# A GRU behind a long convolution on one core: one of four channel chunks of the convolution goes from VectorE to ScalarE and GpSimd

## What is computed

```python
def reference(x, cond_2048, L1_cond_W_ih, L1_cond_W_hh, L1_cond_b_ih, L1_cond_b_hh):
    ...
    def cell(h, x):
        gi = x @ W_ih + b_ih
        gh = h @ W_hh + b_hh
        i_r, i_z, i_n = jnp.split(gi, 3, axis=-1)
        h_r, h_z, h_n = jnp.split(gh, 3, axis=-1)
        r = jax.nn.sigmoid(i_r + h_r)
        z = jax.nn.sigmoid(i_z + h_z)
        n = jnp.tanh(i_n + r * h_n)
        h_new = (1.0 - z) * n + z * h
        return (h_new, h_new)
    ...
    x = x + _L0_cond_ref(x, cond_2048[:, None, :])
    x = x + _L1_cond_ref(cond_2048, x, L1_cond_W_ih, L1_cond_W_hh, L1_cond_b_ih, L1_cond_b_hh)
    return x
```

## Time and profile before

| | |
|---|---|
| median of 3 runs | 1025.09 us (1024.73 to 1025.14) |
| profiled execution, span | 1023.1 us |
| TensorE busy | 1015.2 us, 99% |
| VectorE busy | 865.7 us, 85% |
| ScalarE busy | 398.5 us, 39% |
| GpSimd busy | 237.9 us, 23% |
| granted TensorE clock, mean | 1.000 |

### The profile page before, as it was taken

One profiled execution on the slowest core, in us unless ns is written; L12 is line 12 of the kernel. 1 busy time (PEld: TensorE's weight loads), 2 busy tenths in 40 slices (PEclk: granted clock), 3 DMA queues, 4 the chain that ended last, 5 costly groups with the idle time before them and its releaser, 6 DMA issues.

```text
span 1023.1 us, 58102 instructions
## 1 busy us (share of the span) xinstructions
PE 1015.2 (99%) x24838; PEld 808.1 (79%) x24838; DVE 865.7 (85%) x2851; ACT 398.5 (39%) x1816; POOL 237.9 (23%) x784
## 2 busy tenths in 40 slices
PE   8999999999999999999999999999999999999997
PEld 5878888888787888888888888888888888888875
DVE  7788888888898888888888898888888887777555
ACT  5334333433433343333434333333433343333433
POOL 3222222222222222222222222222222222222222
PEclk9999999999999999999999999999999999999999
DMA  8721001010100101001010010101001000000000
GB/s 297 72 35 39 19 21 31 15 36 19 29 25 12 35 19 34 24 11 36 15 39 19 15 36 11 39 19 28 22 15 35 14 29 16 11 29 4 20 19 13
DMA packets 66994, 32.07 MB, mean 31 GB/s; under 512 B 44464, under 2 KB 65584, under 8 KB 66736
## 3 DMA queue, kind: packets, MB, share of 16 engines
q1 hardware_dynamic: 66304, 28.25, 10.8%
q10 hardware_dynamic: 432, 0.11, 0.0%
HBM read 19.86 MB, written 8.49 MB: 28 GB/s over the span
## 4 chain that ended last, share of the span: by engine, by line
PE 97%; issue 1%; POOL 1%; DVE 0%; DMA 0%; ACT 0%; DVEq 0%; POOLq 0%
PE pg L334 65%; PE pg L324 32%; POOL tz L283 1%; PE pcv L362 0%; DMA cnd<-cond 0%; DVE hp L570 0%; DVE gn L549 0%; POOL nzh L296 0%; DVE an L557 0%; POOL cpad L273 0%; POOL nzh L280 0%; POOL cpad L275 0%; POOL rz L278 0%; POOL zcp L279 0%; ACT nzh L472 0%
## 5 line engine op out<-in xcount | busy, mean ns | idle before, releaser
L334 PE MATMUL pg<-whh,hp 128*32 128x192 f32 x16368 | 713.0, 326 | 2.2 <-ACT whh L461 1.1
L334 PEld LDWEIGHTS pg<-whh,hp 128*32 128x32 f32 x16368 | 531.2, 110 | 137.7 <-DVE hp L570 4.2
L324 PE MATMUL pg<-wih,x 128*32 128x192 f32 x8192 | 381.3, 326 | 0.0
L296 POOL TENSOR_TENSOR nzh<-rz,hp 128x32 f32<-128x32 f32 x512 | 158.2, 309 | 780.1 <-ACT rz L467 780.1
L467 ACT ACTIVATE rz<-gt 128x64 f32<-128x64 f32 x512 | 136.3, 266 | 483.7 <-DVE gt L545 458.9
L324 PEld LDWEIGHTS pg<-wih,x 128*32 128x32 f32 x8192 | 265.5, 110 | 65.8
L512 DVE SCALAR_TENSOR_TENSOR x<-xb,cnd,x 128x512 f32<-128x512 f32 (+1 forms) x420 | 294.8, 702 | 7.9
L570 DVE TENSOR_TENSOR_SCAN hp<-zcp,nzh 128x96 f32<-128x96 f32 x512 | 173.6, 339 | 41.6 <-ACT nzh L472 41.3
L545 DVE STREAM_TRANSPOSE gt<-pg 128x128 f32<-128x128 f32 x512 | 160.2, 313 | 49.4 <-PE pg L334 42.0
L557 DVE TENSOR_TENSOR_SCAN an<-rz,gn 128x64 f32<-128x64 f32 x512 | 149.2, 291 | 51.9 <-ACT rz L467 51.7
L472 ACT ACTIVATE nzh<-an 128x32 f32<-128x32 f32 x512 | 120.6, 236 | 126.9 <-DVE an L557 126.9
(11 more groups left out here) (47 smaller groups left out, 47.4 us busy)
## 6 DMA issues: line engine op xcount, KB each, us to landing
xb<-x SPq DMA_DIRECT2D x96, 94.0 KB, 2.0
out<-x SPq DMA_DIRECT2D x60, 128.0 KB, 1.9
wih<-w_ih SPq DMA_DIRECT2D x4, 768.0 KB, 8.0
whh<-w_hh SPq DMA_DIRECT2D x4, 768.0 KB, 14.6
xw<-x SPq DMA_DIRECT2D x24, 64.0 KB, 3.5
xb<-x SPq DMA_DIRECT2D x16, 62.0 KB, 1.9
tz<-taps SPq DMA_DIRECT2D x12, 64.0 KB, 3.5
xs<-x SPq DMA_DIRECT2D x1, 512.0 KB, 4.7
```

What stands on the lines that cost most here:

```text
L296: pool.tensor_tensor(nzh[:, f, ::2, :, 1], chunks(rz[:, f, 1, :, 1]), h_of(t - 1, slice(f * CH, (f + 1) * CH)), ALU.mult).then_inc(s_zh[f], 1)
L324: i = pe.matmul(pg[m % Q][f][D * j:D * (j + 1), RZ:END], x1_of(c, 2 * m, 2 * m + 2), wih[:, c, :, :].rearrange("p (g k) (j d) -> p j g k d ...
L334: i = pe.matmul(pg[t // 2 % Q][f][D * j:D * (j + 1), 0:IN], hp[:, t % 2, 2 * c + 1 - t % 2:2 * c + 3 - t % 2, :, 1].rearrange("p u b -> p ...
```

## The change

Chunk 3 (`SHARED = C - 1`) of the seven windows leaves VectorE. ScalarE makes the product of the shifted x by the tap's column into one of two new buffers `prod` (`weigh`, line 480 of the changed kernel), and GpSimd adds it into x1 (`gather`, line 313). There are 16 of each per window, so 112 of each in all, and VectorE keeps 48 per window. `weigh` stands at the end of a step on ScalarE, behind the seeds; `gather` at the end of a step on GpSimd, one step later (`t - 1`). TensorE's products wait for the sums as well. The fourth chunk's input is loaded at the window's start, the other three a little more spread out. In the changed kernel `recur` is line 361, `product` 351, `scan_h` 611, z·h 319, `add_out` 298, `long` 553.

```diff
+        prod = [sb(f"prod{i}", [P, W2 * B]) for i in range(2)]
...
-        EVERY = [(lag, c) for c in range(C) for lag in range(K)]
+        EVERY = [(lag, c) for c in range(C - 1) for lag in range(K)]
+        SHARED = C - 1
...
-            at = SPANS[k][0] + W2 // C * c
+            at = SPANS[k][0] + (0 if c == SHARED else W2 // SHARED * c)
...
                 if i == 0 and k >= 2:
-                    sp.wait_ge(s_long, len(EVERY) * (k - 2) + K * (c + 1))
+                    if c == SHARED:
+                        sp.wait_ge(s_prod, K * (k - 1))
+                        sp.wait_ge(s_sum, K * (k - 2) + 1)
+                    else:
+                        sp.wait_ge(s_long, len(EVERY) * (k - 2) + K * (c + 1))
...
+            def gather(k, lag):
+
+                q = K * k + lag
+                a, b = LONG[k]
+                n = (b - a) * B
+                pool.wait_ge(s_prod, q + 1)
+                if lag == 0 and b > KEEP:
+                    for s in range(max(a - KEEP, 0) // TB, (b - 1 - KEEP) // TB + 1):
+                        pool.wait_ge(s_out[s], 16 * C)
+                if lag:
+                    pool.wait_ge(s_sum, q)
+                o = x1_of(SHARED, a, b)
+                now = window(k)[:, SHARED, (K - 1) * B:(K - 1) * B + n]
+                pool.tensor_tensor(o, prod[lag % 2][:, 0:n], o if lag else now, ALU.add).then_inc(s_sum, 1)
...
                     if f == 0 and t:
                         add_out(t - 1)
+                for k, steps in enumerate(SPANS):
+                    for lag in share(K, steps, t - 1):
+                        gather(k, lag)
...
                         pe.wait_ge(s_long, len(EVERY) * sum(a <= 2 * m for a, _ in LONG))
+                    pe.wait_ge(s_sum, K * sum(a <= 2 * m for a, _ in LONG))
...
+            def weigh(k, lag):
+
+                q = K * k + lag
+                n = (LONG[k][1] - LONG[k][0]) * B
+                if lag == 0:
+                    act.wait_ge(s_xb[k][SHARED], 16 * PIECES)
+                if q >= 2:
+                    act.wait_ge(s_sum, q - 1)
+                act.activation(prod[lag % 2][:, 0:n], window(k)[:, SHARED, (K - 1 - lag) * B:(K - 1 - lag) * B + n],
+                               ACT.Copy, scale=cnd[:, SHARED, K - 1 - lag:K - lag]).then_inc(s_prod, 1)
...
                         seed(t // 2 + Q, f)
+                for k, steps in enumerate(SPANS):
+                    for lag in share(K, steps, t):
+                        weigh(k, lag)
```

More of the change, by code:

```diff
@@ L112, in build @@
         s_long = sem("s_long")
+        s_prod = sem("s_prod")
+        s_sum = sem("s_sum")
         s_cv = sem("s_cv")
```

## The result

The changed kernel takes 1097.34 us (1096.98 to 1097.68, 3 runs) against 1025.09: a ratio of 1.0704, 95% interval 1.0689 to 1.0719. The forecast was 1095, 1070 to 1120. The profiled span is 1095.6 us, 72.5 above that of before.

The account below looks back on a forecast made before the run. TensorE's work alone was taken to set the pace. Profiled span 1023.1 + 2.0 to the runs' median + 70 us for held scans and windows' ends = 1095 us, range 1070 to 1120, given 0.80.

Parts of the forecast that it names:

- TensorE sets the pace, and relieving VectorE is worth nothing: Whole step: TensorE, busy 99%, takes 3.90 us; removing 112 VectorE operations, at most 83 us of busy time, was worth 0.
- ScalarE's product at 0.63 to 1.02 us, worth nothing: End of each odd step on ScalarE: the added 128x512 product fits the 1.50 us gap after the seeds; worth 0.
- G, the length of a sum: GpSimd's added 128x512 sum, one per even step: forecast to take 1.21 us, between 1.03 and 1.38.
- my two pairs of rows: Small GpSimd operations, 128x32 to 128x64: 1.59 and 2.38 ns per element, extended to 1.03 and 1.38 us per full-size sum.
- Half-size: GpSimd's smaller sums in the last window: forecast at 0.62, 0.70 or 0.78 us.
- The sum starts 0.28 us before the scan of h and is first: Even steps: GpSimd's sum holds the SBUF reading path; VectorE's second-half scan ends 0.20 us after it, TensorE resumes 0.05 later.
- Loss G - 0.64: Even steps, TensorE waiting for the held scan of h: 0.57 us lost per full-size sum, 0.39 to 0.74.
- TensorE cannot make it up: Even steps: TensorE recovers none of the 0.57 us it waits for the held scan of h.
- the last window's sums: Even steps of the last window: 15 half-size sums of 0.70 us, each losing 0.70 - 0.64 us.
- The wait at the windows' ends, 2.64 us: Seven window ends: TensorE's first product waits for the same step's sixteenth sum, 2.64 us, 2.13 at the last.
- 51 + 1 + 18 = 70 forecast: Whole kernel, us: full-size sums holding the scan, the last window's half-size sums, and the seven waits at windows' ends.
- SyncE's two new waits: Input loads on SyncE and DMA: both waits on sums of the window two before, done over 30 steps earlier; worth 0.

## Why the prediction was right, point by point

- *TensorE sets the pace, and relieving VectorE is worth nothing.* Right: the run without sums has 71 us less of VectorE's work and a ratio of 0.9994.
- *ScalarE's product at 0.63 to 1.02 us, worth nothing.* Right: 0.71 us (708 ns for the full size), and the same run shows it free.
- *G, the length of a sum, 1.21 us, between 1.03 and 1.38.* It was 1.28. The estimate from the Trainium skill's "GPSIMD Engine Reference", 1.26, was closer than the middle of my two pairs of rows. Half-size: 0.73, forecast 0.70.
- *The sum starts 0.28 us before the scan of h and is first; the scan ends 0.20 after it; TensorE 0.05 later.* Right: 0.28, 0.22, 0.05, by the timeline above. That it is the reading, and the first to come, was argued then from overlaps of 0.04 to 0.06 us; the runs with the memset, the copy and the added wait show it.
- *Loss G - 0.64, 0.57 us per sum.* Mis-sized in its form. With the G measured, it would have been 0.64; the steps lose 0.51. The wait in the timeline is that of the loads, 0.68 us; the matmuls, which run behind the loads, idle for only 0.30. After the wait 40 loads take 1.46 us, 0.037 each, not 0.040, so TensorE makes up about 0.15 us. My "TensorE cannot make it up" was too strict. A sum taken too short and a loss taken too long partly cancelled: 90 x 0.57 = 51 forecast, 46 measured. For the same reason the last window's sums cost nothing, not 0.06 each.
- *The wait at the windows' ends, 2.64 us.* The mechanism was right, and the size too where the clock held: 2.62 at the first end, 2.08 at the last (forecast 2.13). Two errors nearly cancel in that size as well: the loads waited 2.77 and 2.23 us there, and TensorE made up about 0.15. **The term that was too small is the other five**, 4.10 to 4.30 us. I counted the stall and not that the granted clock can fall with it: 25.8 us for all seven instead of 18.
- *The sum.* 51 + 1 + 18 = 70 forecast; 46 + 0 + 25.8 and 0.7 elsewhere, 72.5 measured. So the total is nearer than its terms are, by luck: they were off by 5 us one way and 8 the other.
- *SyncE's two new waits, "on sums of the window two before, done over 30 steps earlier".* One of them is on products, and by the program the last of these is made 27 steps before the loads that wait for it (for the third window, step 43 against step 70). Worth 0 all the same.

## What to carry to other kernels

An engine with time to spare is not free to use: GpSimd was busy for 23%, and its sum of 1.28 us still made a scan that the recurrence waited for 0.86 us longer (1.22 instead of 0.36), because both read SBUF and the sum came 0.28 us earlier; 0.51 us of that was lost in each such step. Before moving work to it, look in the timeline for the instruction of VectorE with two operands in SBUF that starts next, ask which of the two comes first and how much room the later one has, and if need be let the moved work wait for it: here one such wait and a start two steps earlier turned 7% slower into no change. A sum of half the size, 0.73 us, in the same place cost nothing in the last window, where the room covered the hold. And if the engine that sets the pace has no idle time that the relieved engine causes, the best that a relief can bring is what the experiment without sums shows, nothing.

## What was not expected of the hardware

TensorE's granted clock fell to 1.2 GHz around a single idle stretch of 2.4 us of its matmuls, in a stream that was otherwise nearly full, and this cost 1.5 to 1.7 us each time. It did so at five of seven windows' ends, after 2.42 or 2.48 us each; at the first, after 2.42 us too, and at the last, after 1.88, it did not. What decides between the first and the second was not tried. With matmuls on zeros in the stretch the clock stood at its upper level at all seven ends (mean 1.000).
